# Seven recurrence steps to a batch of the last attention, and its last projection and a first norm moved between the products of the last feed-forward

## The chip, the cores and the metric

One Trainium2 chip, one core. The time is device microseconds for one launch of the whole kernel; the median over runs is what is compared, and one further execution was profiled.

## What is computed

Four small transformer blocks run one after the other on x (16 batches of 100 rows, 256 columns) with a context of 16 batches of 361 rows: attention and feed-forward blocks (stages s0, c0, f0, s1, f1, c1, f2), then a block with a recurrence and a cross attention, and last a scoring of the context against the rows (not touched). The block that the change concerns is, cut to what matters:

```python
def step(h_prev, zt_gt):
    z_t, g_t = zt_gt
    gate = jax.nn.sigmoid(z_t @ Wgz + bgz + h_prev @ Wgh + bgh)
    h_tilde = (1.0 - gate) * h_prev + gate * z_t
    h_t = h_tilde + g_t * h_prev
    return (h_t, h_t)
_, h_seq_T = jax.lax.scan(step, h0, (z_T, gamma_T))      # 100 steps, all 16 batches in each
scores = jnp.einsum('bshd,bmhd->bhsm', qh, kh) / jnp.sqrt(jnp.asarray(hd, x.dtype))
probs = jax.nn.softmax(scores, axis=-1)
mem_out = jnp.einsum('bhsm,bmhd->bshd', probs, vh).reshape(B, S, D) @ Awo + abo
x_res = x + (h_seq + mem_out + v * 0.1)
x_norm2 = _rms(x_res, norm2_scale)
ffn = jax.nn.gelu(x_norm2 @ Wf1 + bf1) @ Wf2 + bf2
return x_res + ffn
```

## The kernel before, in words

All engine programs are written out by hand as Python generators, one program for each engine (`program_pe`, `program_act`, `program_dve`, `program_pool`, `program_sp`), which walk the same lists so that each engine's order agrees with the others'. Semaphore counts are found in a first, counting build.

**The last attention, c2.** It has 8 heads of 32 columns and runs over 16 batches, in 4 groups of 4. What an engine does in one batch is the string `ORDER["c2"]` (line 145). Its letters: `T0`..`T3` are the score products whose row maxima are taken (L482), `m0`..`m7` those maxima on VectorE (L1314), `X` the turning of the maxima (L490 on TensorE, L1325 on VectorE), `R0`..`R3` the scores again with the maxima subtracted (L509, L512) and their exponentials on ScalarE (L1005), `P0 P1` probabilities times values of the batch before (L537), `n0 n1 n2` its normalisation on VectorE (two reciprocals at L1362, a product at L1370), `K0 K1` keys of the batch after next (L444), `V0 V1 V2` values of the next batch (L399). T, V and X belong to the next batch, so the last batches have fewer of them: batch 14 has no K, batch 15 has no T, V, K or X.

**The recurrence.** `S` is the first part of one recurrence step, `D` the second. On TensorE (`pe_steps`, L802 and L805) `S` is 14 short products of 48 columns; they need the parts of the state that VectorE wrote last. On VectorE `S` is the sum of the three parts (L1625), `D` the six operations that make the new state and split it in three bf16 parts (L1631 to L1642). ScalarE does a tanh between (L1192), GpSimd prepares two operands (L1769, L1770). The string has six `S` and six `D`, so 16 batches hold 96 of the 100 steps; the other four run behind the attention, in a loop of their own (`for _ in step: pass`).

**Fillers.** `F` takes the next slot of `pe_fill` / `act_fill` / `dve_fill`: in group g the output projection of group g-1 (`pe_post`, from slot `POST_AT`, 2) and the queries of group g+1 (`pe_pre`, from slot `PRE_AT`, 4). With two `F` in a batch, slots 2 and 3 are in the second batch of a group, slots 4 and 5 in the third. All slots lie at the same two places in the string.

**Behind it.** After the four steps `together(pe_close, pe_post, pe_chain)` runs the values of batch 15, the output projection of group 3, and the norm r2 of group 0: a sum with the recurrence's output (`dve_recurrent`, L1443), squares on ScalarE (L1020), their mean on TensorE (L399), a square root on ScalarE (L1026), a reciprocal (L1422) and a scaling (L1433) on VectorE. Then comes the last feed-forward, ft (`pe_feed`): for each of 4 groups eight up products (L399, each followed by one slot of `pe_beside`) and two down products (L714). In ft the slots hold the norm r2 of the next group. The up products of group 0 need r2 of group 0.

**Loads.** SP loads the first target rows when the values of batch 15 are through (L1819, 12 transfers), and then, when the last projection of c2 is through, the second weight of ft, 1 MB over the place of c2's weights (L1822); the down products wait for it (`"w f2 tail"`).

Of the kernel before, what the change touches and what calls it, by code (L numbers as in the profile page):

```python
# [14 lines left out]
B, S, C, D, FF = 16, 100, 361, 256, 1024  # L15
# [3 lines left out]
NG = B // GB  # L19
# [98 lines left out]
for a in ATT.values():  # L118
# [27 lines left out]
}  # L146
POST_AT = {"s0": 2, "c0": 0, "s1": 2, "c1": 0, "c2": 2}
PRE_AT = {"s0": 7, "c0": 4, "s1": 4, "c1": 3, "c2": 4}
NORM_OF = {"s0": "n1", "c0": "n2"}
AFTER = {"f0": "c0", "f1": "s1", "f2": "c1"}  # L150
NORM_AFTER = {"f0": "n3", "f2": "r1"}
OPENS = {"f0": "s1", "f1": "c1"}
PROBS_KEPT = 6
ROUND_AT = {}
# [21 lines left out]
def build(nc, book, x_in, ctx_in, vec_in, const_in, src_in, w0_in, w1_in, w2_in, tw_in, out, spill):  # L176
    known = book.known
    with ExitStack() as ctx:
# [463 lines left out]
        def pe_fill(pe, t, g):  # L642

            parts = []
            if t == "s0":
                parts.append(later(1, pe_unload(pe, g)))
            if g or t == "c0":
                parts.append(later(POST_AT[t], pe_post(pe, *((t, g - 1) if g else ("s0", NG - 1)), lin[t])))
            elif t == "s1":
                parts.append(pe_chain(pe, "n3", NG - 1, lin[t]))  # L650
            if g + 1 < NG:
                parts.append(later(PRE_AT[t], pe_pre(pe, t, g + 1)))
            elif t == "s0":
                parts.append(later(12, pe_open(pe, "c0")))
            return together(*parts)
# [30 lines left out]
        def pe_beside(pe, of, g):  # L686

            parts = []
            if g == 0 and of in AFTER:
                parts.append(pe_close(pe, AFTER[of]))  # L690
                parts.append(later(2, pe_post(pe, AFTER[of], NG - 1, lin[""])))
            elif g and of in NORM_AFTER:
                parts.append(pe_chain(pe, NORM_AFTER[of], g - 1, lin[""]))
            elif of == "ft" and g + 1 < NG:
                parts.append(pe_chain(pe, "r2", g + 1, lin[""]))
            if g + 1 == NG and of in OPENS:
                parts.append(later(4 if of == "f0" else 0, pe_open(pe, OPENS[of])))
            return together(*parts)
# [161 lines left out]
        def program_pe(pe):  # L860
# [39 lines left out]
            pe_attention(pe, "c2", step)  # L900
            for _ in step:
                pass
            for _ in together(pe_close(pe, "c2"), pe_post(pe, "c2", NG - 1, lin[""]), later(2, pe_chain(pe, "r2", 0, lin[""]))):
                pass
            pe_feed(pe, "ft")
            for b in range(2):
                pe_target_scores(pe, b)
# [177 lines left out]
        def act_fill(act, t, g):  # L1085
            parts = []
            if t == "s0":
                parts.append(later(1, act_unload(act, g)))
            if g or t == "c0":
                of, og = (t, g - 1) if g else ("s0", NG - 1)  # L1090
                if of in NORM_OF:
                    parts.append(later(POST_AT[t] + 3, act_chain(act, NORM_OF[of], og)))
            elif t == "s1":
                parts.append(act_chain(act, "n3", NG - 1))
            if g + 1 < NG:
                parts.append(later(PRE_AT[t], act_pre(act, t, g + 1)))
            elif t == "s0":
                parts.append(later(12, act_open(act, "c0")))
            return together(*parts)
# [21 lines left out]
        def act_beside(act, of, g):  # L1121
            parts = []
            if g == 0 and of in AFTER:
                if ATT[AFTER[of]]["e"] == 2:
                    act_second(act, AFTER[of], B - 1)
                if AFTER[of] in NORM_OF:
                    parts.append(later(5, act_chain(act, NORM_OF[AFTER[of]], NG - 1)))
            elif g and of in NORM_AFTER:
                parts.append(act_chain(act, NORM_AFTER[of], g - 1))
            elif of == "ft" and g + 1 < NG:  # L1130
                parts.append(act_chain(act, "r2", g + 1))
            if g + 1 == NG and of in OPENS:
                parts.append(later(4 if of == "f0" else 0, act_open(act, OPENS[of])))
            return together(*parts)
# [103 lines left out]
        def program_act(act):  # L1238
# [31 lines left out]
            step = act_steps(act)  # L1270
            act_attention(act, "c2", step)
            for _ in step:
                pass
            for _ in act_chain(act, "r2", 0):
                pass
            act_feed(act, "ft")
            for b in range(2):
# [203 lines left out]
        def dve_fill(dve, t, g):  # L1481
# [2 lines left out]
                parts.append(later(POST_AT[t], dve_post(dve, *((t, g - 1) if g else ("s0", NG - 1)))))  # L1484
            elif t == "s1":
                parts.append(dve_chain(dve, "n3", NG - 1))
            if g + 1 == NG and t == "s0":
                parts.append(later(12, dve_open(dve, "c0")))
            return together(*parts)
# [23 lines left out]
        def dve_beside(dve, of, g):  # L1513
# [3 lines left out]
                parts.append(later(2, dve_post(dve, AFTER[of], NG - 1)))  # L1517
            elif g and of in NORM_AFTER:
                parts.append(dve_chain(dve, NORM_AFTER[of], g - 1))
            elif of == "ft" and g + 1 < NG:  # L1520
                parts.append(dve_chain(dve, "r2", g + 1))
            if g + 1 == NG and of in OPENS:
                parts.append(later(4 if of == "f0" else 0, dve_open(dve, OPENS[of])))
# [149 lines left out]
        def program_dve(dve):  # L1673
# [38 lines left out]
            step = dve_steps(dve)  # L1712
            dve_attention(dve, "c2", step)
            for _ in step:
                pass
            for _ in together(dve_close(dve, "c2"), dve_post(dve, "c2", NG - 1), later(2, dve_chain(dve, "r2", 0))):
                pass
            dve_feed(dve, "ft")
            for b in range(2):
# [260 lines left out]
```

## Time and profile before

| | us |
|---|---|
| median of 3 runs | 1707.24 (1707.0 to 1708.08) |
| the profiled execution, its own time | 1706.5 |
| its span, first to last instruction | 1704.8 |
| TensorE busy | 1606.2 (94%) |
| VectorE busy | 800.9 (47%) |
| ScalarE busy | 662.3 (39%) |
| GpSimd busy | 163.5 (10%) |
| mean granted TensorE clock | 0.966 of full |

The span is the profile's own; the time that is compared has 1.7 us more around it. Busy shares are means over stages. TensorE's row counts a short product that waits in the pipe like a long one, so a busy TensorE can still be slow: look at the granted clock and at the starts of the instructions.

### The profile page before, as it was taken

Reading aid. Unit: us, or ns where it says so; the run is one execution under the profiler, and the core shown is the slowest. Engines: PE = TensorE matmul, PEld = TensorE weight load, DVE = VectorE, ACT = ScalarE, POOL = GpSimd, SP = SyncE. Lnnn points to the kernel's source line nnn. Section 1 sums busy time; section 2 is a strip of 40 time slices with the busy share of each in tenths; the row PEclk is TensorE's granted clock in tenths of the full one; section 3 lists DMA queues with packets and bytes.
Section 4 is the critical chain, followed back from the end, with each engine's and each line's share of the span. In section 5 each row is a group of like instructions: output and inputs, shape, how many; then the busy total and the mean of one; then the engine's idle time right before and its main releaser. Section 6 shows DMA issues by size and latency. Waiting matters only on the chain.

```text
span 1704.8 us, 32358 instructions
## 1 busy us (share of the span) xinstructions
PE 1606.2 (94%) x14092; PEld 1050.6 (62%) x14092; DVE 800.9 (47%) x1768; ACT 662.3 (39%) x1321; POOL 163.5 (10%) x350
## 2 busy tenths in 40 slices
PE   7998899999999999999999999999999999859998
PEld 6655456666655556555677765554677777735565
DVE  1567757666542256211233332235576777642132
ACT  2455446556453443111333321234343434313333
POOL 1333300100000000000000000000121112100000
PEclk9899999999999999999999999998799999979999
DMA  4211000000000010000100000000000000020021
GB/s 147 95 45 45 10 26 2 1 2 1 2 26 0 0 75 1 21 1 0 75 1 1 2 26 0 0 7 1 26 2 2 2 2 2 2 73 0 0 85 59
DMA packets 19197, 37.13 MB, mean 22 GB/s; under 512 B 2000, under 2 KB 17136, under 8 KB 17776
## 3 DMA queue, kind: packets, MB, share of 16 engines
q1 hardware_dynamic: 19056, 35.07, 6.2%
q8 instruction: 110, 1.80, 0.4%
q14 instruction: 31, 0.25, 0.0%
HBM read 33.43 MB, written 1.64 MB: 21 GB/s over the span
## 4 chain that ended last, share of the span: by engine, by line
PE 84%; DVE 10%; ACT 4%; issue 1%; DMA 0%; SPq 0%; DVEq 0%; ACTq 0%
PE psum L399 38%; PE psum L714 10%; PE psum L444 8%; PE psum L537 8%; PE psum L512 7%; DVE maxima L1314 2%; PE psum L482 2%; PE psum L805 2%; ACT probs L1005 2%; PE psum L509 2%; PE psum L802 1%; DVE denoms L1352 1%; PE psum L833 1%; PE psum L846 1%; DVE q_then_o L1357 1%; PE psum L814 1%
## 5 line engine op out<-in xcount | busy, mean ns | idle before, releaser
L1314 DVE TENSOR_REDUCE maxima<-psum 100x2 f32<-100x722 f32 (+3 forms) x332 | 243.6, 757 | 122.3 <-PE psum L482 102.7
L399 PE MATMUL psum<-x_resid,weights 128*128 128x400 f32 x832 | 292.8, 502 | 3.9 <-ACT probs L1005 1.6
L1005 ACT ACTIVATE probs<-psum 128x800 f32<-128x800 f32 (+3 forms) x240 | 171.5, 748 | 152.6 <-PE psum L512 150.8
L399 PEld LDWEIGHTS psum<-x_resid,weights 128*128 128x128 f32 x832 | 155.7, 190 | 120.1 <-issue 4.2
L714 PE MATMUL psum<-weights 128*128 128x400 f32 x512 | 175.0, 499 | 0.7 <-DVE maxima L1314 0.7
L399 PE MATMUL psum<-weights,ctx_t 128*128 128x256 f32 (+1 forms) x576 | 158.8, 400 | 1.4 <-ACT weights L926 0.7
L444 PE MATMUL psum<-ctx_t,weights 128*128 128x361 f32 x384 | 145.5, 506 | 1.1 <-DVE weights L1536 0.8
L714 PEld LDWEIGHTS psum<-weights 128*128 128x128 f32 x512 | 97.2, 190 | 75.1 <-DVE maxima L1314 0.8
L509 PE MATMUL psum<-max_rows,ones_bf 32*128 32x200 bf16 (+7 forms) x1152 | 129.1, 232 | 9.5 <-ACT probs L1005 5.6
L976 ACT ACTIVATE values<-psum 128x256 f32<-128x256 f32 (+2 forms) x176 | 67.6, 384 | 157.5 <-PE psum L399 112.7
L399 PEld LDWEIGHTS psum<-weights,ctx_t 128*128 128x128 f32 (+1 forms) x576 | 100.0, 187 | 40.9 <-issue 10.5
L926 ACT ACTIVATE weights<-psum 128x400 f32<-128x400 f32 (+2 forms) x80 | 38.1, 476 | 213.1 <-PE psum L399 213.1
L537 PE MATMUL psum<-probs,values 128*32 128x100 f32 (+5 forms) x3328 | 112.9, 254 | 0.3 <-DVE q_then_o L1370 0.2
L512 PE MATMUL psum<-q_then_o,keys 32*128 32x100 f32 (+4 forms) x1280 | 105.1, 289 | 0.0
L1536 DVE TENSOR_TENSOR weights<-psum,weights 128x400 f32<-128x400 f32 x64 | 36.8, 574 | 137.9 <-PE psum L399 119.6
L537 PEld LDWEIGHTS psum<-probs,values 128*32 128x32 f32 (+5 forms) x3328 | 85.6, 114 | 22.8 <-issue 19.6
L512 PE MATMUL psum<-q_masked,keys 32*128 32x200 f32 (+2 forms) x1024 | 97.3, 341 | 0.0
L444 PEld LDWEIGHTS psum<-ctx_t,weights 128*128 128x128 f32 x384 | 71.6, 200 | 40.2 <-issue 13.1
L512 PEld LDWEIGHTS psum<-q_then_o,keys 32*128 32x128 f32 (+4 forms) x1280 | 91.8, 184 | 2.6
L1743 POOL TENSOR_TENSOR q_masked_bf<-q_then_o,ones 128x200 bf16<-128x200 f32 x48 | 25.4, 536 | 702.2 <-ACT q_then_o L926 553.7
L509 PEld LDWEIGHTS psum<-max_rows,ones_bf 32*128 32x128 bf16 (+5 forms) x1152 | 65.1, 117 | 34.6 <-DVE maxima L1314 11.5
L926 ACT ACTIVATE weights<-psum,vectors 128x400 f32<-128x400 f32 x80 | 46.3, 593 | 102.9 <-PE psum L399 102.7
(145 smaller groups left out, 2257.7 us busy)
## 6 DMA issues: line engine op xcount, KB each, us to landing
weights<-in_w SPq DMA_DIRECT2D x2, 3072.0 KB, 9.7
staged<-in_ctx SPq DMA_DIRECT2D x32, 128.0 KB, 2.1
values<-in_ctx SPq DMA_DIRECT2D x32, 128.0 KB, 2.2
weights<-in_w SPq DMA_DIRECT2D x3, 1024.0 KB, 4.7
weights<-in_src SPq DMA_DIRECT2D x1, 2368.0 KB, 13.3
weights<-in_w SPq DMA_DIRECT2D x1, 2048.0 KB, 8.3
weights<-in_tw SPq DMA_DIRECT2D x2, 1024.0 KB, 4.9
staged<-in_ctx SPq DMA_DIRECT2D x16, 105.0 KB, 2.2
```

Of the source, the lines that this page charges most:

```text
L399: i = nc.tensor.matmul(PS[0:rows, bk, 0:n], lhs, rhs, start=k == 0, stop=k == len(terms) - 1)
L444: i = nc.tensor.matmul(PS[:, bk + m, 0:C], w(WN[t][1], c, m * P, (m + 1) * P), CT[:, b, c, :], start=c == 0, stop=c == DC - 1)
L482: i = nc.tensor.matmul(PS[0:S, bk + d, 0:C], queries_bf(t, b, i0 + d, c, e), keys_bf(t, b, i0 + d, c), start=True, stop=True)
L509: nc.tensor.matmul(PS[0:kn, bk + d, m * n:(m + 1) * n], ONEB[tile_rows(t, i0 + d), 0:kn], MB[tile_rows(t, i0 + d), b % 2, c * n:(c + 1) * ...
L512: i = nc.tensor.matmul(PS[0:kn, bk + d, m * n:(m + 1) * n], keys_of(t, b, i0 + d, c, k0, kn), queries_of(t, b, i0 + d, c), start=False, st ...
L537: mm = nc.tensor.matmul(PS[tile_rows(t, i), bk, o:o + S], lhs, probs_of(t, b, i, c, kc, kn, e), start=kc == 0, stop=kc == lastk)
L714: i = nc.tensor.matmul(PS[:, bk, 0:N], w(wd, k, m * P, (m + 1) * P), hidden[:, k, :], start=k == 0, stop=k == 7)
L926: nc.scalar.activation(out, PS[0:rows, bank(use), 0:n], func, **kw).then_inc(act_results, mark("act", point or f"{use} out"))
L976: nc.scalar.activation(dst, src, ACT.Copy).then_inc(act_results, mark("act", f"{use} out"))
L1005: nc.scalar.activation(PT[0:kn, k % PROBS_KEPT, :, 0:n], PS[0:kn, bk:bk + 2, 0:n], ACT.Exp).then_inc(act_results, mark("act", f"{t} p{b} { ...
L1314: nc.vector.reduce_max(top, src, AX).then_inc(dve_results, mark("dve", f"{t} m{b} {j}"))
L1536: nc.vector.tensor_tensor(H[:, m, :], PS[:, bank(up), 0:N], U[:, m % 2, :], ALU.mult).then_inc(dve_results, mark("dve", f"{of} u{g} {m}"))
```

## The change

It adds a seventh `S` and `D` to the string of c2 (behind `X`) and a third `F` (in front of `n1`), moves the projection's first slot from 2 to 3, and takes out the code between c2 and ft. The values of batch 15, the output projection of group 3 go into ft's first group through `AFTER`; the norm r2 of group 0 goes into the slots of c2's last group, from slot 7. ScalarE's and VectorE's programs are changed in the same way as TensorE's.

```diff
-    "c2": "S T0 D R0 m0 m1 F S P0 D T1 m2 R1 S P1 m3 T2 D V0 m4 S m5 D F R2 R3 n0 T3 S K0 V1 m6 D m7 S n1 D K1 X V2 n2",
+    "c2": "S T0 D R0 m0 m1 F S P0 D T1 m2 R1 S P1 m3 T2 D V0 m4 S m5 D F R2 R3 n0 T3 S K0 V1 m6 D m7 S F n1 D K1 X S V2 D n2",
 }
-POST_AT = {"s0": 2, "c0": 0, "s1": 2, "c1": 0, "c2": 2}
+POST_AT = {"s0": 2, "c0": 0, "s1": 2, "c1": 0, "c2": 3}
 PRE_AT = {"s0": 7, "c0": 4, "s1": 4, "c1": 3, "c2": 4}
-AFTER = {"f0": "c0", "f1": "s1", "f2": "c1"}
+AFTER = {"f0": "c0", "f1": "s1", "f2": "c1", "ft": "c2"}
 NORM_AFTER = {"f0": "n3", "f2": "r1"}
+TAIL_AT = 7
...
+            if t == "c2" and g + 1 == NG:
+                parts.append(later(TAIL_AT, pe_chain(pe, "r2", 0, lin[t])))
...
-            elif of == "ft" and g + 1 < NG:
+            if of == "ft" and g + 1 < NG:
                 parts.append(pe_chain(pe, "r2", g + 1, lin[""]))
...
             pe_attention(pe, "c2", step)
             for _ in step:
                 pass
-            for _ in together(pe_close(pe, "c2"), pe_post(pe, "c2", NG - 1, lin[""]), later(2, pe_chain(pe, "r2", 0, lin[""]))):
-                pass
             pe_feed(pe, "ft")
...
```

## Rows read from the trace of the kernel before

**Rows 1.** The page's first part: busy time of TensorE over the whole span.

```profile
PE 1606.2 (94%) x14092; PEld 1050.6 (62%) x14092; DVE 800.9 (47%) x1768; ACT 662.3 (39%) x1321; POOL 163.5 (10%) x350
```

**Rows 2.** Busy time by stretch (us, PE, PEld, DVE, ACT, POOL, granted clock, DMA share, GB/s).

```profile
1203.51:1466.60 263.09, 253.37 (x3910) 195.77 (x3911) 188.29 (x762) 102.77 (x244) 51.40 (x184) 0.96 0.02 6
1296.89:1318.48 21.59, 21.22 (x298) 15.54 (x298) 14.40 (x57) 7.01 (x18) 3.66 (x13) 1.00 0.01 2
1318.48:1337.34 18.86, 18.49 (x290) 14.04 (x290) 13.29 (x55) 8.11 (x20) 3.60 (x13) 1.00 0.01 2
1466.60:1483.64 17.04, 13.90 (x274) 11.30 (x274) 13.16 (x55) 5.76 (x15) 3.13 (x12) 1.00 0.01 2
1483.64:1499.87 16.23, 9.91 (x252) 8.71 (x253) 9.94 (x47) 3.95 (x10) 3.20 (x12) 0.86 0.01 2
1530.60:1556.35 25.75, 25.75 (x69) 14.37 (x70) 5.29 (x6) 8.63 (x13) 0.00 (x0) 0.89 0.00 1
1556.35:1579.30 22.95, 22.95 (x70) 13.03 (x69) 6.07 (x7) 8.55 (x13) 0.00 (x0) 1.00 0.00 0
```

**Rows 3.** TensorE in order of time: starts of the steps in batch 11 (start, duration).

```profile
1411.40 0.25 PE L802 MATMUL psum<-weights,ident_bf 128*128 128x48 bf16 x1
...
1413.95 0.25 PE L802 MATMUL psum<-weights,ident_bf 128*128 128x48 bf16 x1 [0.38 <-DVE h_parts L1642]
...
1417.22 0.25 PE L802 MATMUL psum<-weights,ident_bf 128*128 128x48 bf16 x1
...
1420.22 0.25 PE L802 MATMUL psum<-weights,ident_bf 128*128 128x48 bf16 x1
...
1422.77 0.25 PE L802 MATMUL psum<-weights,ident_bf 128*128 128x48 bf16 x1 [0.21 <-DVE h_parts L1642]
...
1425.42 0.25 PE L802 MATMUL psum<-weights,ident_bf 128*128 128x48 bf16 x1
...
1425.91 1.46 PE L444 MATMUL psum<-ctx_t,weights 128*128 128x361 f32 x4
1427.21 0.25 PE L490 MATMUL psum<-constants,maxima 100*128 100x100 f32 x1
1427.30 1.03 PE L399 MATMUL psum<-weights,ctx_t 128*105 128x256 f32 x4
1428.20 0.25 PE L802 MATMUL psum<-weights,ident_bf 128*128 128x48 bf16 x1
```

**Rows 4.** VectorE in order of time: a step with the reciprocal n1, in batch 10.

```profile
1409.52 0.77 DVE L1362 RECIPROCAL denoms<-psum 128x100 f32<-128x100 f32 x1
...
1411.10 0.23 DVE L1642 TENSOR_TENSOR h_parts<-scan_state,h_parts 128x32 bf16<-128x32 f32 x1
```

**Rows 5.** TensorE in order of time: two of the four steps behind the attention.

```profile
1502.58 0.25 PE L802 MATMUL psum<-weights,ident_bf 128*128 128x48 bf16 x1 [1.90 <-DVE h_parts L1642]
...
1505.29 0.25 PE L802 MATMUL psum<-weights,ident_bf 128*128 128x48 bf16 x1 [1.90 <-DVE h_parts L1642]
```

**Rows 6.** All engines in order of time: the norm in front of the last feed-forward.

```profile
1524.26 1.28 ACT L1026 ACT_TABLE_LOAD   x1
...
1524.34 1.58 PE L399 MATMUL psum<-t,ones_mean 128*128 128x400 f32 x4 [2.31 <-ACT t L1020]
...
1526.58 2.65 DVE L1422 RECIPROCAL t<-t 128x400 f32<-128x400 f32 x1 [2.91 <-ACT t L1026]
...
1530.60 1.67 PE L399 MATMUL psum<-t,weights 128*128 128x400 f32 x2 [4.68 <-DVE t L1433]
```

**Rows 7.** The chain that ended last: values, 48 products (start, us).

```profile
1469.79 1.17 PE psum L537 x48
```

**Rows 8.** Busy time by stretch again: batch 4, and three microseconds at its end.

```profile
1278.37:1296.89 18.52, 17.75 (x282) 13.84 (x282) 13.12 (x55) 7.14 (x18) 3.61 (x13) 0.91 0.01 3
1291.00:1294.00 3.00, 3.00 (x8) 1.92 (x7) 1.64 (x8) 1.03 (x3) 0.99 (x3) 0.51 0.00 0
```

**Rows 9.** DMA issues between 1512 and 1530 us (KB each, us to landing).

```profile
weights<-in_tw SPq DMA_DIRECT2D x1, 1024.0 KB, 4.9
```

More of the change, by code:

```diff
@@ L1094, in act_fill @@
                 parts.append(act_chain(act, "n3", NG - 1))
+            if t == "c2" and g + 1 == NG:
+                parts.append(later(TAIL_AT, act_chain(act, "r2", 0)))
             if g + 1 < NG:
@@ L1129, in act_beside @@
                 parts.append(act_chain(act, NORM_AFTER[of], g - 1))
-            elif of == "ft" and g + 1 < NG:
+            if of == "ft" and g + 1 < NG:
                 parts.append(act_chain(act, "r2", g + 1))
@@ L1272, in program_act @@
             for _ in step:
-                pass
-            for _ in act_chain(act, "r2", 0):
                 pass
@@ L1486, in dve_fill @@
                 parts.append(dve_chain(dve, "n3", NG - 1))
+            if t == "c2" and g + 1 == NG:
+                parts.append(later(TAIL_AT, dve_chain(dve, "r2", 0)))
             if g + 1 == NG and t == "s0":
@@ L1519, in dve_beside @@
                 parts.append(dve_chain(dve, NORM_AFTER[of], g - 1))
-            elif of == "ft" and g + 1 < NG:
+            if of == "ft" and g + 1 < NG:
                 parts.append(dve_chain(dve, "r2", g + 1))
@@ L1714, in program_dve @@
             for _ in step:
-                pass
-            for _ in together(dve_close(dve, "c2"), dve_post(dve, "c2", NG - 1), later(2, dve_chain(dve, "r2", 0))):
                 pass
```

## The prediction

> **What bounds the kernel now.** The page first: TensorE is busy 94% of the span [rows 1], so what lengthens or stalls its own stream costs time. Then the stretches [rows 2]: batches 0 to 13 of the last attention (c2) take 263.09 us with TensorE busy 253.37 (96%), batches 14 and 15 take 17.04 and 16.23 with 13.90 and 9.91 busy. So the holes are at the end, and the dense part is nearly full. The order of time inside a batch says what sets its length. The starts of the steps in a plain batch [rows 3] cut it into six pieces of 2.55, 3.27, 3.00, 2.55, 2.65 and 2.78 us, 16.80 in all. Two of them (1 and 4, both 2.55) end in a wait for VectorE's state parts, 0.38 and 0.21 us: there the recurrence, not TensorE's work, is the bound. The other four are work. Behind the attention the steps have nothing beside them: each waits 1.90 us and comes 2.71 us after the last [rows 5].
>
> So one step can't follow another in less than 2.55 us. Six steps fit in 16.80 us with little waiting; seven need at least 17.85, and only if work lies evenly between them.
>
> **The change, part by part.** All sums are in the profiled execution's time, 1706.5 us (span 1704.8); the median is 0.74 above it.
>
> *The seventh step, batches 0 to 13.* It stands behind X and in front of V2. Piece 6 (step, K1, X, V2: 0.49, 1.30, 0.09, 0.90 by their starts [rows 3]) loses V2 and is 1.88 us of work, but the next step has to wait for a state that the reciprocal n1 (0.77 us) delays: in batch 10 such a state was written at 1411.10 plus 0.23, 2.67 us after its step at 1408.66 (estimate for that start: 2.74 before 1411.40) [rows 3, 4]. So piece 6 is about 2.74. The new piece 7 is a step and V2, 1.39 us of work, and takes the floor, 2.55. A plain batch becomes 16.80 - 2.78 + 2.74 + 2.55 = 19.31, **2.51 us longer**, though the step itself is 0.49 us of TensorE. Fourteen batches: +35.1. Queued behind the new step: on GpSimd the mask of the batch after next, which waits 2.55 us more and is wanted only behind the next batch's first step; on ScalarE, V2's copy; both have room, at nothing (without it, their own half microsecond each).
>
> *The third F.* Projection and queries cost 4.79 and 2.06 us over a plain batch now (21.59 and 18.86 [rows 2]), as they fill the two waits. They are 16 and 8 products of 0.337 us (22.95 us for the 68 of a feed-forward group [rows 2]), 5.4 and 2.7. Afterwards the second half of the queries lies in piece 6, whose 0.86 us of waiting it fills. By the waits filled this saves 0.45 us in group 0 and 0.1 each in groups 1 and 2: -0.7. Sum to the start of batch 14: +34.4, so 1501.0 instead of 1466.60.
>
> *Batch 14.* It holds steps 98 and 99 alone. TensorE's 13.90 us less four steps of 0.49 is 11.9; with a wait for the maxima, behind which 1.05 us of the new r2 sum stands on VectorE, I take 12.3 until R0 of batch 15, 1513.3. Of its 17.04 us, 4.7 go.
>
> *Batch 15, the four steps, the code behind.* Products R0, P0, R1, P1 follow without steps: P is 1.17 [rows 7]; piece 2 less step and P is 1.61, of which R is some 1.3. That is 4.95, then the mean's four products 1.35: 1519.6. From there the norm's path is known: 0.66 us to the reciprocal and 4.02 from its start to the first product [rows 6], so the **first up product at 1524.3** instead of 1530.60. The square root now needs ScalarE to change its table away from the exponential and back, 1.28 us each [rows 6]; R2's and R3's exponentials stand behind it and end some 9.2 us after R0, 3 us before the values of batch 15 want them, since an up product and the norm are ahead. I cost that at nothing; without this cover it is 1.3 to 2.6.
>
> *The first group of ft.* It takes up two P of 1.17 (2.34) and 16 projection products (5.4), before done behind c2. A group at full clock is 22.95 [rows 2]: 30.7, end at 1555.0, against 1556.35 before. **So far -1.4.** VectorE's waits for these products hold up only the norm of group 1, due 20 us later. The weight for the down products is asked for when the projection ends, some 13.3 us into the group, behind twelve target loads that are through by then; it lands 4.9 us later [rows 9], at 18.3, and the down products start at 19.9. Cost nothing; if the loads are slower, 0 to 2.
>
> *The clock, before ft.* The first group of ft took 25.75 us at a mean granted clock of 0.89, the next 22.95 at 1.00 [rows 2]: 2.8 us lost, after a hole of 4.68 us [rows 6]. Afterwards the mean is followed by R2 and R3, short products of some 0.9 us, and a hole of 3.8. The bounds are 0 and 2.8; nearer to what was seen, I take +2.0. Sum: +0.6.
>
> *The clock, inside c2.* Batch 4 took 18.52 us instead of 16.80 [rows 8, 3]. Its last products were granted 0.51 (1.2 of 2.4 GHz) for three microseconds, with TensorE busy throughout [rows 8]; before it lay piece 4, which is steps and short 32-row products and a wait of 0.3 us. That is one fall in fourteen batches, 1.7 us each. The change makes a worse place of the same kind in every batch: from the end of V2 to the next P now lie a wait of 1.15 us, a step, T0, R0, a wait, a step, some 4.2 us in place of 3.0, with nothing in them but steps, 32-row products and waits. How often the clock falls there no row tells: none, or in every batch (14 falls, +24). The one fall was at a shorter place of this kind, which speaks for some; I take **three more, +5.1**, since a clock that fell at every such place would have fallen oftener before. Sum: +5.7, which is 1706.5 + 5.7 + 0.74, rounded to **1713 us**.
>
> The Trainium skill (TensorE: Matmul & The Clock Gate, HAM oscillation) ties such falls to long idle gaps between bursts of products. The waits of the new piece are far shorter than those, and by that rule the clock falls nowhere more inside c2, which gives the second rival's time. The trace disagrees in one place, batch 4, where the clock fell after waits of at most 0.3 us.
>
> **The rivals.**
> - *No more falls* (chance 0.22). The sum is then +0.6, or 1708.0 with the 0.74. For it: thirteen of fourteen batches kept the clock, and batch 14, with TensorE busy 13.90 of 17.04, was granted 1.00 throughout. Against it: batch 4.
> - *Falls in most batches* (0.15): the stretch between K1 and V2 trips it too. Eight falls, 13.6 us, give 1721.
> - *Faster* (0.09): the floor itself is lower in the dense part. If n1's reciprocal slips into ScalarE's tanh, piece 6 is 2.55 and fourteen batches save 2.7 us; if then the clock holds before ft and the one fall of batch 4 is gone, the sum is -1.4 - 2.7 - 1.7 = -5.8, or 1701.5. It decides at 0.25 us a batch. Against it: piece 6 with its reciprocal fits 2.74 in batch 10 [rows 4].
> - *Late weight, or late exponentials* (0.04): the down products or the values wait, +2 on the forecast, 1715.
> - That the change doesn't do what it says I can exclude: the lists are the order of the engines' streams, and nothing else holds the 100 steps. What could be is that the seventh step costs only its 0.49 us of TensorE: -28 us. The floor of 2.55 us, seen in two pieces of each batch, excludes it.
>
> **How the numbers follow.** Forecast 0.50, the others 0.22, 0.15, 0.09, 0.04. The measurement tells about 0.2%, 3.4 us, from no change: slower begins at 1710.7, faster ends at 1703.8. The forecast's own spread (one to five more falls, 1709.7 to 1716.5) leaves 0.03 of its 0.50 under 1710.7. Slower: 0.47 + 0.15 + 0.04 = 0.66; same 0.22 + 0.03 = 0.25; faster 0.09. The range takes in the second case and reaches halfway into the third, 1705 to 1720; the faster case and the worst of the falls are left out.
>
> **What would show it.** In the profile after: steps 2.55 us apart in the new piece and about 2.74 in piece 6, plain batches of 19.3 us, batch 14 starting near 1501, the last step near 1503.6, the first up product near 1524 and the second group of ft near 1555 plus falls. Falls show as a granted clock near 0.5 at the start of piece 2. If a plain batch is 17.3 us the floor is wrong and the kernel is some 28 us faster; if it is over 20, another wait has entered piece 7 (X's turn or V2's bank). If TensorE waits at the down products of ft's first group, it is the weight.

## The result, and the profile after

| | before | after |
|---|---|---|
| median of 3 runs | 1707.24 us | 1723.73 us (1720.26 to 1726.64) |
| the profiled execution, its own time | 1706.5 | 1720.26 |
| its span | 1704.8 | 1718.5 |

The kernel is slower, as forecast, but by more than the range held: the ratio is 1.0094, interval [1.0064, 1.0125], where the forecast was 1.0034 and the range ended at 1.0075.

The page's first part, of the kernel after. Against [rows 1], TensorE is busy 11 us longer in a span that is 13.7 us longer; the share of 94% is the same and tells nothing of the cause.

```profile
PE 1617.2 (94%) x14092; PEld 1055.5 (61%) x14092; DVE 802.5 (47%) x1768; ACT 663.4 (39%) x1322; POOL 163.6 (10%) x350
```

Busy time by stretch, with the columns of [rows 2]: batches 0 to 13; plain batch 10; plain batch 7 and the 4.3 us of its second piece; batch 14; batch 15's products up to the first up product; the first group of ft; the second.

```profile
1205.19:1513.70 308.51, 276.61 (x4107) 210.92 (x4107) 208.54 (x861) 106.99 (x259) 58.76 (x212) 0.92 0.02 5
1427.13:1446.46 19.33, 16.92 (x295) 13.37 (x296) 14.48 (x62) 7.35 (x18) 4.17 (x15) 1.00 0.01 3
1358.63:1379.08 20.45, 18.18 (x296) 14.43 (x296) 14.69 (x62) 7.35 (x18) 4.18 (x15) 0.92 0.01 2
1361.20:1365.50 4.30, 4.30 (x88) 3.88 (x88) 2.67 (x10) 0.86 (x2) 0.51 (x2) 0.68 0.02 6
1513.70:1526.32 12.62, 11.70 (x217) 9.00 (x218) 9.30 (x29) 4.64 (x10) 0.51 (x2) 1.00 0.01 3
1526.32:1537.78 11.46, 7.55 (x173) 6.05 (x173) 4.90 (x5) 7.40 (x9) 0.00 (x0) 1.00 0.01 1
1537.78:1570.11 32.33, 32.33 (x181) 18.73 (x182) 9.25 (x12) 8.82 (x13) 0.00 (x0) 0.95 0.30 96
1570.11:1593.05 22.94, 22.94 (x70) 13.02 (x69) 6.07 (x7) 8.54 (x13) 0.00 (x0) 1.00 0.00 0
```

Read them as a ledger. Batches 0 to 13 take 308.51 us instead of 263.09, **45.42 more**. From the start of batch 14 to the second group of ft it is 56.41 (1513.70 to 1570.11) instead of 89.75 (1466.60 to 1556.35), **33.34 less**. c2 itself starts 1.68 later, before any edited line. Sum 13.76, the difference of the spans. So 12 of the 13.7 us come from the difference of two large terms. The second came out as forecast (56.41 us, where the forecast's terms add up to 56.0), and the question is why the first is 45.4 and not 34.4.

Batch 10 gives one half of the answer. TensorE in order of time, its pieces 6 and 7 (start, duration; in brackets the wait before it and who ended it):

```profile
1441.14 0.25 PE L805 MATMUL psum<-weights,ident_bf 128*128 128x48 bf16 x1
...
1443.91 0.25 PE L805 MATMUL psum<-weights,ident_bf 128*128 128x48 bf16 x1 [0.74 <-DVE h_parts L1645]
1444.40 1.09 PE L400 MATMUL psum<-weights,ctx_t 128*105 128x256 f32 x4
1446.46 0.25 PE L805 MATMUL psum<-weights,ident_bf 128*128 128x48 bf16 x1 [0.97 <-DVE h_parts L1645]
```

The steps lie 2.77 and 2.55 us apart, both ended by VectorE's state. The batch is 19.33 long, and its granted clock is 1.00. A batch that keeps the clock costs what was forecast.

Batch 7 gives the other half. TensorE at the end of its first piece and in its second:

```profile
1358.63 0.25 PE L805 MATMUL psum<-weights,ident_bf 128*128 128x48 bf16 x1 [0.96 <-DVE h_parts L1645]
...
1360.06 0.43 PE L513 MATMUL psum<-q_then_o,keys 32*128 32x100 f32 x4
1360.37 0.58 PE L513 MATMUL psum<-q_then_o,keys 32*128 32x100 f32 x4
1361.17 0.25 PE L805 MATMUL psum<-weights,ident_bf 128*128 128x48 bf16 x1 [0.23 <-DVE h_parts L1645]
...
1361.91 1.23 PE L538 MATMUL psum<-probs,values 128*32 128x100 f32 x24
1362.91 1.19 PE L538 MATMUL psum<-probs,ones 128*32 128x100 f32 x24
```

The last R0 group takes 0.58 instead of 0.43, and then P's two halves 1.23 and 1.19 us (0.73 and 0.70 at full clock, at 1530.18 in the same execution), with the clock at a mean of 0.68 over the piece: for part of it 1.2 GHz were granted instead of 2.4. The piece is 4.38 us instead of 3.27. Reading the starts of all steps in this way, piece 2 is stretched in batches 4, 6, 7, 8, 11 and 12 (to 4.34 to 4.74), and piece 1, into which the projection's two fillers fall, in batches 5, 9 and 13 (6.54 to 6.59 instead of 4.89). Six times it is 1.1 to 1.5 us, three times 1.7. **Nine falls in fourteen batches**, 12.4 us. With the 34.4 of the forecast, less before's own fall of 1.7 in batch 4, that makes 45.1 of the 45.4.

The end of the kernel came as worked out. All engines in order of time, the norm in front of ft:

```profile
1531.15 1.28 ACT L1027 ACT_TABLE_LOAD   x1
1531.35 1.61 PE L400 MATMUL psum<-t,ones_mean 128*128 128x400 f32 x4
1533.00 0.59 ACT L1027 ACTIVATE t<-psum,eps 128x400 f32<-128x400 f32 x1 [0.56 <-PE psum L400]
1533.61 1.28 ACT L1006 ACT_TABLE_LOAD   x1
1534.91 0.90 ACT L1006 ACTIVATE probs<-psum 105x400 f32<-105x400 f32 x2
1533.63 2.65 DVE L1423 RECIPROCAL t<-t 128x400 f32<-128x400 f32 x1 [1.36 <-ACT t L1027]
1537.78 2.80 PE L400 MATMUL psum<-t,weights 128*128 128x400 f32 x4 [3.91 <-DVE t L1434]
1559.36 10.91 PE L717 MATMUL psum<-weights 128*128 128x400 f32 x32
```

The hole is 3.91 us (3.8 forecast, 4.68 in [rows 6]). The table goes away under the mean and comes back under the reciprocal, 1.28 us each. The first up product, four instructions, takes 2.80 us; the same product at full clock takes 1.51 (e8, at 1550.35). The down products start at 1559.36 without a wait: the weight had landed.

### The profile page after: what moved, and what is told of

Same layout as the page of the kernel before. It is cut to its first block, busy times and chain, and to the rows that moved or that the text cites. A ratio compares the mean times of both kernels' runs of the same rounds, so it can differ in the third digit from the quotient of the medians.

```text
span 1718.5 us, 32351 instructions
## 1 busy us (share of the span) xinstructions
PE 1617.2 (94%) x14092; PEld 1055.5 (61%) x14092; DVE 802.5 (47%) x1768; ACT 663.4 (39%) x1322; POOL 163.6 (10%) x350
## 4 chain that ended last, share of the span: by engine, by line
PE 81%; DVE 12%; ACT 4%; issue 1%; DMA 0%; SPq 0%; DVEq 0%; ACTq 0%
PE psum L400 38%; PE psum L717 10%; PE psum L538 8%; PE psum L445 7%; PE psum L513 6%; DVE maxima L1315 2%; PE psum L483 2%; PE psum L808 2%; PE psum L510 2%; ACT probs L1006 2%; PE psum L805 2%; DVE denoms L1353 1%; PE psum L836 1%; PE psum L849 1%; DVE q_then_o L1358 1%
```

## The experiments

Two theories to begin with. **Clock**: the new stretch of steps, 32-row products and waits makes TensorE's clock fall, and nothing else is wrong with a seventh step beyond its 2.5 us. **Its rival**: the seventh step itself stretches other pieces (a bank, a turn on VectorE), or the end gives back less than it seems. Every ratio below is against runs of the kernel before on the same chip as the experiment, since the kernel before moved from chip to chip too (medians 1708.86 to 1715.01).

### The two halves of the change, each alone

`e1_seven_old_tail` keeps the seven steps and the third F, and puts the old code back behind c2. `e2_six_new_tail` is the kernel before with the values of batch 15 and the last projection moved into ft; the norm r2 of group 0 stands behind the four steps.

```diff
 # e1, against the kernel after
-AFTER = {"f0": "c0", "f1": "s1", "f2": "c1", "ft": "c2"}
+AFTER = {"f0": "c0", "f1": "s1", "f2": "c1"}
...
-            if t == "c2" and g + 1 == NG:
-                parts.append(later(TAIL_AT, pe_chain(pe, "r2", 0, lin[t])))
...
+            for _ in together(pe_close(pe, "c2"), pe_post(pe, "c2", NG - 1, lin[""]), later(2, pe_chain(pe, "r2", 0, lin[""]))):
+                pass
 # e2, against the kernel before
-AFTER = {"f0": "c0", "f1": "s1", "f2": "c1"}
+AFTER = {"f0": "c0", "f1": "s1", "f2": "c1", "ft": "c2"}
...
-            for _ in together(pe_close(pe, "c2"), pe_post(pe, "c2", NG - 1, lin[""]), later(2, pe_chain(pe, "r2", 0, lin[""]))):
+            for _ in pe_chain(pe, "r2", 0, lin[""]):
                 pass
```

> Seven steps to a batch and the third F as in the changed kernel, but values, projection and first norm behind c2 as before. Theory (the loss is the seventh step with the clock's falls, the tail part is a gain): a plain batch of 19.3 us, piece 2 or 1 stretched by 1.1 to 1.7 us in about nine batches, and, since the hole behind c2 comes back (18 us from the values to the first up product at full clock), 4 to 7 us more than the changed kernel: 1725 to 1731. Rival (the tail part costs as much as it gives, since the norm in batch 15 leaves TensorE without work): within 2 us of the changed kernel, 1722 to 1726.

> Six steps to a batch and the four steps behind the attention as before; the values of batch 15 and the last projection in the first group of ft; the first norm stands alone behind the steps. Theory: the first up product comes 8.0 us after the last state, near 1518 instead of 1530.6 of the profiled kernel before, and the first group of ft is 7.7 us longer: 4 to 6 us gained, 1701 to 1704. Rival (products moved between those of ft cost what they cost behind c2, and a longer hole keeps the clock low for longer): 1706 to 1709.

Measured: seven steps with the old end 1737.78 us (4 runs, ratio 1.0148 [1.0117, 1.0178]); six steps with the new end 1710.11 (10 runs, 0.9971 [0.9944, 0.9998]). In e1's trace plain batches without a fall are 19.3 to 19.4 us as in the kernel after, nine batches have a fall, one of them a long one, in which pieces 2 and 3 are 5.73 and 5.23 us instead of 3.27 and 3.00. From the start of batch 14 to ft's second group e1 takes 68.10 us, the kernel after 56.41, which is 11.7 less. But 2.5 of that is one more fall of e1, in batch 14, which takes 15.08 there (1518.72 to 1533.80) instead of 12.62. So the moved work is worth some 9 us in these executions; e1's ratio against the two of the changed kernel (1.0094 above, 1.0109 in e5 below) gives 7 to 9, with intervals that overlap, and e2's ratio 5. The two halves pull against each other: the end gives, the seventh step takes. In e2 the first up product comes at 1527.41, 3.2 earlier than before, although two falls (pieces 2 and 3 of batch 8, 5.51 and 5.23, and 5.38 instead of 3.09 in batch 15) lie ahead of it. Falls belong to six steps as well; they are only rarer.

### Does wide work in the waits keep the clock?

If the clock falls for want of wide products in the new stretch, products that fill the two new waits should keep it; if it falls because TensorE waits, any products should; and if a bank or a turn stretches the pieces, neither does. `e3_wide_fillers` puts two f32 products of 361 columns behind X and two behind V2, `e4_narrow_fillers` 18 bf16 products of 48 columns at each of the same places. The results of these products are not used by anything.

```diff
-    "c2": "... D K1 X S V2 D n2",
+    "c2": "... D K1 X W0 S V2 W0 D n2",
...
+                        elif kind == "W":
...
 # e3
+                            for _ in range(2):
+                                nc.tensor.matmul(PS[:, bk, 0:C], IDENT, CT[:, b, 0, :], start=True, stop=True)
 # e4
+                            for _ in range(18):
+                                nc.tensor.matmul(PS[:, bk, 0:48], IDB[:, :], IDB[:, 0:48], start=True, stop=True)
```

> The changed kernel with two full-width products of 361 columns (0.33 us each, their result is not used) in each of the two waits of TensorE, behind X and behind V2. Theory that the clock falls where a stretch has no wide products: at most three falls in c2, plain batches still 19.3 us (the waits hide the fillers), batches with queries some 0.7 us longer, 1709 to 1714. Theory that it falls where TensorE waits: the same here. Rival (the stretches of piece 2 are no falls but waits for data): no change, 1722 to 1727.

> As e3, but with eighteen products of 48 columns bf16 (the form of the recurrence's own, some 0.64 us together) in each place. If waits as such bring the falls, this cures them like e3: 1709 to 1714. If it is the lack of wide products, the falls stay, eight or more: 1720 to 1727.

Measured: e3 1719.25 us (10 runs, 1.004 [1.0023, 1.0057]), e4 1732.67 (4 runs, 1.0122 [1.0093, 1.0151]). Busy time by stretch, batches 0 to 13 and plain batch 11 of e3:

```profile
1203.71:1508.91 305.20, 294.12 (x4219) 224.32 (x4220) 207.65 (x861) 107.31 (x259) 58.62 (x212) 0.97 0.02 6
1444.77:1464.52 19.75, 19.05 (x304) 14.93 (x304) 14.43 (x62) 7.35 (x18) 4.17 (x15) 1.00 0.01 2
```

And batches 0 to 13 of e4, with the first microsecond of batch 14:

```profile
1204.88:1528.00 323.12, 301.95 (x4630) 236.45 (x4632) 209.03 (x862) 107.43 (x259) 58.62 (x212) 0.89 0.02 5
```

In e3 no piece of batches 1 to 13 has a fall, and their mean clock is 1.00. What keeps its mean over c2 at 0.97 is batch 0, which is at a low clock in the kernel before too. The first row is e3's batches 1 to 13, the second the kernel before's batch 0:

```profile
1229.17:1508.91 279.74, 271.05 (x4013) 206.57 (x4013) 192.33 (x799) 98.68 (x240) 54.03 (x195) 1.00 0.01 2
1203.51:1225.92 22.41, 20.03 (x186) 15.72 (x186) 13.96 (x55) 7.78 (x17) 4.09 (x15) 0.62 0.15 48
```

In e4 nine batches have a fall, three of them long ones (5.59 and 5.20 in batch 2, 5.57 and 5.22 in batch 3, 5.67 and 5.06 in batch 7). TensorE is busy 301.95 of 323.12 us, 93%, more than the 90% of the kernel after (276.61 of 308.51), and yet the clock is at a mean of 0.89, lower than its 0.92. The fairest partner of e4 is e6 of the next part, with two wide products in a single wait. This is plain batch 10 of e4, and TensorE at its two waits:

```profile
1440.38:1459.72 19.34, 17.81 (x331) 14.55 (x332) 14.49 (x62) 7.35 (x18) 4.17 (x15) 1.00 0.01 3
```

```profile
1456.26 0.61 PE L690 MATMUL psum<-ident_bf 128*128 128x48 bf16 x18
1457.17 0.25 PE L812 MATMUL psum<-weights,ident_bf 128*128 128x48 bf16 x1 [0.30 <-DVE h_parts L1652]
...
1459.72 0.25 PE L812 MATMUL psum<-weights,ident_bf 128*128 128x48 bf16 x1 [0.53 <-DVE h_parts L1652]
```

e4 leaves TensorE idle for 1.53 us of a batch and e6 for 1.45 (19.42 less 17.97), nearly the same, and e4 has falls in nine batches where e6 has one. So the sum of the waiting doesn't decide, and it matters what the products in the waits are. That the waits have no part in it isn't shown: e4's products left 0.30 and 0.53 us of the two, e6's leave 0.75 of the first and nothing of the second, and no run filled the wait behind V2 wholly with narrow products. e3 didn't come back to the time without falls because the filler was too long. My expectation had half of its true length, since one f32 product of 361 columns is two instructions, and four of them stretch over 1.2 us (1438.26 to 1439.47 in e6's lines further down): X's place made piece 6 3.12 instead of 2.79, and in the query batches 4.46 instead of 3.22.

### The smallest filler, with the changed kernel beside it

`e5_changed_again` is the kernel after, unchanged, on the chip of `e6_one_filler`, which has only the second of e3's two places, behind V2, whose wait of 0.97 us is the longest of a plain batch.

```diff
-    "c2": "... D K1 X S V2 D n2",
+    "c2": "... D K1 X S V2 W0 D n2",
```

> The changed kernel itself, as the measure for the others on the same chip. The number of falls of the clock in c2 differs from run to run, so its times scatter by some 6 us; on the chip of the first experiments the kernel before was near 1715, and the theory puts this one 14 to 18 us above the kernel before. Rival (the change's loss is a matter of one chip): under 10 us above it.

> The changed kernel with the two wide unused products only behind V2, where they cost 0.08 us a batch instead of 0.44. Theory (a fall needs the long stretch without wide products from V2 to the next P): falls in c2 all gone as with four fillers, plain batches 19.4 us, 5 to 7 us under e3, 9 to 14 us under the changed kernel. Rival (the stretch between K1 and V2 brings falls too): four or more falls stay, within 5 us of the changed kernel.

Measured: e5 1728.37 us (4 runs, 1723.77 to 1738.58, 1.0109 [1.006, 1.0159]); e6 1708.49 (10 runs, 0.9995 [0.9974, 1.0015]), both against 1708.86. Busy time by stretch, e5: batches 0 to 13, plain batch 10, and its second piece.

```profile
1201.40:1523.49 322.09, 290.29 (x4106) 222.06 (x4106) 209.37 (x861) 106.99 (x259) 58.65 (x212) 0.87 0.02 5
1436.33:1456.82 20.49, 18.13 (x296) 14.37 (x296) 14.69 (x62) 7.35 (x18) 4.17 (x15) 0.92 0.01 2
1438.87:1443.29 4.42, 4.42 (x88) 3.91 (x89) 2.76 (x10) 0.80 (x2) 0.57 (x2) 0.68 0.01 4
```

The same for e6, batches 0 to 13 and plain batch 10:

```profile
1203.53:1502.40 298.87, 280.30 (x4163) 214.75 (x4164) 207.57 (x861) 107.10 (x259) 58.64 (x212) 0.97 0.02 6
1420.05:1439.47 19.42, 17.97 (x300) 14.22 (x300) 14.53 (x62) 7.35 (x18) 4.17 (x15) 1.00 0.01 3
```

And what stands in e6's piece 7, TensorE in order of time:

```profile
1437.33 1.09 PE L400 MATMUL psum<-weights,ctx_t 128*105 128x256 f32 x4
1438.26 1.38 PE L690 MATMUL psum<-ctx_t,constants 128*128 128x361 f32 x4
1439.47 0.25 PE L812 MATMUL psum<-weights,ident_bf 128*128 128x48 bf16 x1
```

The filler takes the wait and 0.08 us more. The falls go from twelve of the batches 0 to 13 in e5 (four of them with two stretched pieces: 26.0 us together; batch 14 has one more) to a single one in e6, in piece 5 of batch 4 (4.33 instead of 2.65), where the kernel before had its own [rows 8]. The stretch says the same: 322.09 - 298.87 = 23.2, and 26.0 - 1.7 - 14 x 0.08 = 23.2. (The spans are 23.0 apart: c2 starts 2.1 earlier in e5, and what follows batch 13 takes 1.9 longer.) This is the result that settles the cause of the loss: **with the clock kept, the changed kernel is as fast as the kernel before, within 0.3%, and the falls are the whole of its loss.** What brings a fall is known less well, as the next part shows. e6's batches 0 to 13 are 298.87 - 263.09 = 35.8 us longer than before's, the forecast's 34.4 and fourteen times 0.08.

The price of the falls differs from execution to execution: 12.4 us in the kernel after, 26.0 in e5, which is the same program.

### Spreading the steps evenly

If the falls come of the stretch without wide products, an order in which wide products stand in each piece should keep the clock, and might bring plain batches to the seven floors, 17.85. `e7_level_order` tries it, with one wide filler; `e8_level_and_hole` adds ten wide products in the hole before ft.

```diff
+    "c2": "S T0 P0 D m0 m1 F S P1 T1 D m2 m3 F S R0 V0 D n0 S W0 R1 T2 D m4 S m5 R2 V1 R3 T3 D n1 S m6 K0 V2 D S m7 K1 D F X n2",
 # e8 too
+            for _ in range(10):
+                nc.tensor.matmul(PS[:, SCAN_BANK, 0:C], IDENT, CT[:, 0, 0, :], start=True, stop=True)
             pe_feed(pe, "ft")
```

> Seven steps and the changed kernel's tail, but the work of a batch is laid out anew so that each of the seven pieces holds 1.5 to 2.2 us beside its step, with one wide unused product in front of R1. Theory (the seventh step costs 2.5 us only because the work is uneven and the floor of 2.55 us is paid five times): a plain batch of 18.0 to 18.3 us, no falls, first norm 2 to 3 us earlier: 25 to 32 us under the changed kernel, 10 to 16 us under the kernel before. Rival (any seventh step costs a floor, whatever the order): plain batches stay over 19.2 us.

> e7 with ten wide unused products in front of the last feed-forward, where TensorE has a hole. Theory (the hole lets the clock fall at the start of ft): granted clock 1.00 in ft's first group, 0 to 2 us under e7, less if the hole of e7 is short and the fillers delay the first up product. Rival: no difference or up to 2 us over e7.

Measured: e7 1736.03 us (4 runs, 1718.73 to 1744.3, 1.0133 [1.0061, 1.0205]), e8 1742.39 (4 runs, 1.0178 [1.012, 1.0236]). Both missed. e7's plain batches are 19.5 us, no better: piece 5 is 3.58. TensorE in it, in order of time:

```profile
1441.28 0.25 PE L812 MATMUL psum<-weights,ident_bf 128*128 128x48 bf16 x1
1442.04 0.25 PE L510 MATMUL psum<-max_rows,ones_bf 32*105 32x100 bf16 x2 [0.36 <-ACT probs L1013]
1442.72 1.13 PE L400 MATMUL psum<-weights,ctx_t 128*128 128x256 f32 x4
```

R2 waits 0.36 us for the exponential of R1, which now stands just one piece ahead, and two R, V1 and T3 are more work than a floor. e7's profiled execution is the fastest of its four and has stretched pieces in two batches (3.43 and 3.54 in batch 3, 5.01 and 4.32 in batch 6). e8 is the same program up to the end of c2, and its trace has them in five batches, 1, 3, 5, 7 and 10, mostly over pieces 5 and 6 (5.03 and 4.31 instead of 3.58 and 2.70 in batch 10). Busy time of these two pieces there, from 1446.00 on:

```profile
1446.00:1455.30 9.30, 8.94 (x67) 6.08 (x68) 4.68 (x18) 3.62 (x8) 1.56 (x5) 0.63 0.00 1
```

This speaks against a simple form of the first theory: between the wide filler and V1, where the low clock begins to show, lie 3.0 us of short products and one wait of 0.36 (1439.69 to 1442.72 in e7), no more than the 3.0 of the kernel before, and the falls are many and long. So the length of a stretch without wide products doesn't foretell them by itself; what else it takes, no run here separates.

The ten products of e8 were 6.2 us (1544.18 to the first up product at 1550.35), again twice what I meant, and they found no hole: in this order R2 and R3 of batch 15 fill the wait for the norm, and in e7 the first up product comes at 1536.24 right behind them. They did bring the first group of ft to full clock, 30.62 us (1550.35 to 1580.97) instead of e7's 32.34 (1536.24 to 1568.58), a gain of 1.7 for 6.2. An even order as such is not refuted; this one is.

### A version that is faster than both

What e1 and e2 left: the gain lies at the end, and it doesn't need the seventh step. `e9_six_new_tail_wide` is e2 with wide fillers in the last waits. `e10_norm_first_wide` and `e11_norm_first` keep everything of the kernel before, values of batch 15 and projection in their old place, but let VectorE do the recurrence's sum for the norm before the normalisation of batch 15, and TensorE the mean before the projection, so that the projection's products cover the square root and the reciprocal; e10 has e9's fillers, e11 none.

```diff
 # e11, against the kernel before
-            for _ in together(pe_close(pe, "c2"), pe_post(pe, "c2", NG - 1, lin[""]), later(2, pe_chain(pe, "r2", 0, lin[""]))):
-                pass
+            for c in range(DC):
+                pe_values(pe, "c2", B - 1, c)
+            pe_var(pe, "r2", 0, lin[""])
+            for m in range(DC):
+                pe_out(pe, "c2", NG - 1, m, lin[""])
...
+            dve_recurrent(dve, 0)
+            dve_normalise(dve, "c2", B - 1)
+            dve_scale(dve, "r2", 0)
+            for m in range(DC):
+                dve_out(dve, "c2", NG - 1, m)
```

> e2 (six steps, values and last projection in ft) with wide unused products in the waits of batches 14 and 15, between the four steps and around the norm. Theory (besides the moved work, the low clock at the end costs 0.16 us a step and some 3 us at ft's start): steps 2.55 us apart to the end, first up product at full clock, 3 to 6 us under e2's median of 1710 less the chip's own difference: 8 to 12 us under the kernel before. Rival (fillers take what they give): within 2 us of e2 relative to the kernel before, 3 to 5 us under it.

> Six steps, nothing moved into ft; behind the steps the norm r2 of group 0 comes first on VectorE, and the values of batch 15 and the two projection products stand in TensorE's waits for it; wide unused products as in e9. Theory (what is long behind c2 is the norm's chain of 8 us waiting behind the projection, not the products): first up product 11 us after the last step and no products added to ft, 12 to 17 us under the kernel before. Rival (the chain's own length decides, so that it matters little what stands in it): like e9.

> e10 without any filler. Theory: 7 to 11 us under the kernel before, the rest to e10 being the clock in batch 15, the four steps and ft's first group. Rival (the fillers give nothing): equal to e10.

Measured on one chip: e9 1709.19 us (10 runs, 1.0007 [0.9991, 1.0024]), e10 1700.84 (10 runs, 0.9958 [0.9938, 0.9977]), e11 1696.36 (4 runs, 0.9927 [0.9906, 0.9947]). TensorE in order of time, e11:

```profile
1515.78 1.97 PE L399 MATMUL psum<-t,ones_mean 128*128 128x400 f32 x4 [2.03 <-DVE q_then_o L1373]
1517.54 2.85 PE L399 MATMUL psum<-q_then_o,weights 128*128 128x400 f32 x4
1522.92 1.51 PE L399 MATMUL psum<-staged,weights 128*128 128x400 f32 x4
1524.26 5.54 PE L399 MATMUL psum<-t,weights 128*128 128x400 f32 x16
1536.35 10.91 PE L714 MATMUL psum<-weights 128*128 128x400 f32 x32
```

The hole of 4.68 us in [rows 6] is gone: the up products start at 1524.26 right behind the projection, 6.3 earlier than before, and with the clock kept. Their group ends at 1547.10 (the down products' start and the next group's 10.75 later), 22.84 long against 25.75 [rows 2], another 2.9. Together 9.2, and the span is 9.3 shorter. e11's first group of ft:

```profile
1524.26:1547.10 22.84, 22.84 (x70) 12.93 (x68) 6.07 (x7) 8.55 (x13) 0.00 (x0) 1.00 0.20 70
```

e11 gained more than the 7 to 11 us it was expected to (13.4 under the kernel before), e9 and e10 less (nothing and 8.9, for 8 to 12 and 12 to 17). The fillers of e9 and e10 were too long: in both the last steps lie 3.00 us apart, where bare ones need 2.71 [rows 5], and the batches 14 and 15 take 37.0 us instead of 33.3.

`e12_norm_first_light` is e11 with fillers that fit (two products in each of the last steps' waits, one or two in those of batches 14 and 15 and ahead of the mean), and with the mean in a bank that doesn't wait for the normalisation.

```diff
 # e12, against e11
...
+            for n in range(4):
+                next(step)
+                pe_wide(pe, lin[""], 2 if n < 3 else 0)
...
-            pe_var(pe, "r2", 0, lin[""])
+            pe_wide(pe, flow, 2)
+            pe_var(pe, "r2", 0, flow)
```

> e10 with fillers of the right length (one of them is two instructions of 0.33 us, so that e10's were twice as long as its waits allow): two in each wait of a step, one in the shorter ones, and the norm's mean in a bank that doesn't wait for the normalisation of batch 15 (1.4 us in e11). Theory: steps 2.55 us apart to the end, first group of ft at full clock, 2 to 4 us under e11's distance to the kernel before: 15 to 18 us under it. Rival (a filler in the state's path costs what the clock gives): 11 to 14 us under it, as e11.

Measured: 1693.71 us (7 runs, 1692.35 to 1704.53, 0.9913 [0.9882, 0.9943]). TensorE in order of time:

```profile
1507.05 1.46 PE L662 MATMUL psum<-ctx_t,constants 128*128 128x361 f32 x4
...
1513.24 1.58 PE L399 MATMUL psum<-t,ones_mean 128*128 128x400 f32 x4
...
1520.03 5.54 PE L399 MATMUL psum<-t,weights 128*128 128x400 f32 x16
```

Busy time by stretch, the last three steps of e11:

```profile
1500.85:1508.96 8.11, 2.42 (x43) 2.03 (x43) 4.21 (x22) 0.69 (x3) 1.52 (x6) 0.50 0.00 0
```

And of e12:

```profile
1501.47:1509.11 7.64, 5.85 (x55) 3.45 (x55) 4.23 (x22) 0.69 (x3) 1.53 (x6) 1.00 0.00 0
```

The granted clock is 0.50 without the fillers and 1.00 with them, and the steps are 2.55 us apart instead of 2.70. The mean has no wait, and the first up product is at 1520.03. The span, 1691.3, is 4.2 under e11's. Between the ratios of e11 and e12 the intervals overlap, so that the fillers help beyond e11 is shown by this pair of traces and not by the times.

## Why the prediction was right or wrong

- **The seventh step, floor and pieces.** Right. 19.31 for a plain batch, measured 19.33; piece 6 2.74, measured 2.77; piece 7 2.55, measured 2.55. Neither GpSimd's mask nor V2's copy on ScalarE showed up in a wait of batch 10.
- **The third F.** Right in size: e6, whose falls are known one by one, puts the whole of batches 0 to 13 at the forecast's 34.4 within 0.3 us.
- **Batch 14.** 12.3 forecast, 12.62 measured. **From R0 to the first up product** 11.0, measured 11.46.
- **The first group of ft.** 30.7 at full clock and +2.0 for the clock, 32.7; measured 32.33, with a mean clock of 0.95. The weight cost nothing, as said.
- **Late exponentials.** They did stand behind two table loads, at 1534.91, and no wait of TensorE came of it.
- **The clock inside c2. This is the step that failed**: the term "three more, +5.1", four falls with the one of before. Nine falls came in the profiled execution, 12.4 us, and twelve batches with falls, 26.0 us, in another of the same program. Of the mechanism the text had the place right (from V2's end over the steps and T0, R0 to P, showing at piece 2), and the size of one fall, 1.1 to 1.7 us against 1.7. What it had wrong is the number. The reason given for three, "a clock that fell at every such place would have fallen oftener before", took the rate of the old order over to the new one as though the two were of the same kind; the runs show one fall in fourteen batches before, and nine to twelve batches with falls afterwards. Two readings under it were wrong as well. The low clock of batch 4 lies in piece 5 (K0's products 2.53 us instead of 1.46 at 1290.30), and its last products are at full clock again, so that the one fall known stood behind R2, R3 and T3 and not at the place that the change lengthens (the line below, of the kernel before). And "thirteen of fourteen batches kept the clock" leaves out batch 0, at a mean of 0.62; it is twelve. The text also missed that a fall can be a long one, some 4.4 us over two pieces. The profiled execution took 8.0 us more than the 1712.2 of its sum: 5.6 for falls beyond the forecast's four, 1.7 for c2's later start, which no term held, and 0.7 for everything else. The median lies a further 3.5 us above this execution instead of the 0.74 taken over from before; no trace shows where, but in e5 more falls made the difference between two executions. The rival "falls in most batches" had eight falls and 1721, and came nearest; it deserved more than 0.15, even though its own reason, that the stretch between K1 and V2 brings falls too, is not borne out: e6 leaves that stretch as it is, and the falls go. The upper end of the range should have reached over it, since the text itself worked out fourteen falls at +24 and then left them out.

```profile
1290.30 2.53 PE L444 MATMUL psum<-ctx_t,weights 128*128 128x361 f32 x4
```

- **Small slips in the sums.** 1706.5 + 0.6 + 0.74 is 1707.8 and not 1708.0, and the spread of one to five more falls is 1709.5 to 1716.3. The "products" of 0.337 us are instructions, two to an f32 product; the sums hold, since they count these throughout.
- **The other rivals.** "No more falls" is what e6 makes by adding wide products, at the time of the kernel before. The faster rival's shorter piece 6 did not come. The seventh step for only its own 0.49 us was rightly excluded.
- **The Trainium skill's rule** (TensorE: Matmul & The Clock Gate, HAM oscillation), which ties falls to long idle gaps, would have had no more falls, with the time of the rival of that name. The runs disagree with it here: falls came in nine to twelve batches, where the longest wait inside a plain batch is 0.97 us, and e4, with TensorE busy 93%, has a clock of 0.89 over c2.

Open points: why the falls take some batches and leave others, and differ between executions of one program. c2's start differs by a few microseconds between executions (1205.19 in the kernel after, 1201.40 in e5, the same program), but no run moves it by itself. The fall in piece 5 of batch 4 comes back at the same piece in e6, e11 and e12 (4.33 or 4.34 us) and isn't there in e2, e9 and e10. And no rule for the falls came out of these runs that also holds for e8.

## What to carry to other kernels

Beside the busy share, look at the granted clock of every stretch of TensorE's stream; in this kernel short products and waits in a row cost more through the clock than through their own time, and one fall seen before a change that lengthens such a stretch is a warning, not a rate. If a recurrence's floor leaves a wait, a wide product whose result nobody uses can be cheaper than leaving it (e6), but only at a length taken from a trace, and at a place that the trace of the very order shows (one in front of R1 didn't help in e7 and e8). And before moving work into a later stage to cover a norm, see whether the norm's chain can go ahead of work that is there already: reordering two engines' programs (e11) gave more than the whole change.

## What the hardware showed that I hadn't expected

- The falls depend on what the products are, and not only on whether TensorE is busy: with 18 products of 48 bf16 columns in each wait the clock had a mean of 0.89 over c2, with two f32 products of 361 columns in one of the two waits 0.97, at nearly the same idle time in a batch (1.53 and 1.45 us).
- Most falls have one of two sizes: 1.1 to 1.7 us in one piece (3.27 to 4.4), and 4.1 to 4.7 us over two (3.27 and 3.00 to 5.5 and 5.2).
- The same program has nine such batches in one execution and twelve in another; its times scatter from 1720 to 1739 us over seven executions. A difference of 0.2% can't be read from three runs of a kernel in this condition.
- The floor of a recurrence step hangs on the clock too, short as its products are: 2.70 us at a granted clock of 0.50 (e11), 2.55 at 1.00 (e12), with VectorE and ScalarE busy for the same time in both (4.21 and 4.23, 0.69 and 0.69 us over three steps).
